# A state-space scan on pairs of channel halves, rows of C read from device memory, and two softplus steps on GpSimd

## The chip, the cores and the metric

The kernel runs on one core of a Trainium2 chip. The metric is the device time of one execution, in microseconds.

## The reference

The input x is four sequences of 512 tokens with 128 channels (2048 columns of 128). Six blocks follow one another, each x + f(LayerNorm(x)): a gated feed-forward net, a state-space mixer, the feed-forward net again, a mixture of experts (64 experts, 8 per token), attention with 8 heads, and the experts again. The change is in the mixer:

```python
xz = x @ in_proj_w.T                       # 2 x 256 channels
x_ssm, z = split(xz)
xc = silu(causal_depthwise_conv4(x_ssm) + conv_b)
xp = xc @ x_proj_w.T                       # 1 + 16 + 16 values per token: dt_r, B, C
dt = softplus(dt_r @ dt_proj_w.T + dt_proj_b)
dA = exp(dt[..., None] * -exp(A_log))      # 256 channels x 16 states
dBx = dt[..., None] * B[:, :, None, :] * xc[..., None]
h_t = dA_t * h_(t-1) + dBx_t               # 512 steps, from 0 in each sequence
y_t = sum over the 16 states of h_t * C_t
y = y + xc * D
out = y * silu(z) @ out_proj_w.T
```

## The kernel before, in words

The kernel is written out by hand for each engine: five instruction streams with semaphores between them. Channels lie on the 128 partitions, tokens along the free dimension. The mixer works on one sequence ("block" i, 0 to 3) of 512 tokens at a time, and its 256 channels are two halves m of 128 partitions.

For a block the work is 16 states n times two halves m, 32 items q = 2n + m. An item takes these steps, all 128 x 512:

- TensorE spreads row n of B over the partitions by a selection matrix (L831), into one of four PSUM banks, three items ahead; for m = 1 it spreads a row of C into bank 2 (L838).
- ScalarE makes exp(dt * A) in `m_da` (L1018, records show `ln_t`), and for m = 1 copies the row of C to `m_c` (L1023).
- VectorE multiplies `du` = dt * xc by the row of B in place in PSUM (L1119), one item ahead, and runs the recurrence over the tokens by one scan instruction into `m_h` (L1126).
- GpSimd multiplies `m_h` by the row of C into `m_hc` (L1181, records show `ln_c`).
- TensorE adds that up over n with an identity matrix, in fp32 (L906).

`m_h`, `m_da` and `m_hc` have four slots of one item (`DEEP`). `scan_items` (L717) interleaves with the items of a block: `ahead`, the work for the next blocks (projections, odd taps of the convolution, silus, low halves, softplus), and `finish`, the end of the block before (y with D, gate, output projection, addition to x). Each stands at a fixed q in the order of every engine. In softplus, ScalarE makes |v|, exp(-|v|) and ln(1 + e) (L983, L987, L991), and VectorE adds max(v, 0) (`softplus_end`, L1090) and multiplies by xc (`dt_times_xc`, L1095), both 128 x 1024. In the last block the LayerNorm of the phase behind is begun as well (`early_centre`, `early_inverse`, `early_normalise` on VectorE). After the last item come the y step (L1152), the gate product (L1158), high and low halves (L234, L237), the output projection and the addition to x (L1165). ScalarE changes its function table between silu, exp, ln and square root (`ACT_TABLE_LOAD`).

An f32r product needs a high and a low half of each operand and three matmuls (`mm3`); a low half is a subtraction (L237). The SP queue issues all DMAs; before the change it has nothing to do during the mixer and waits for the phase's end. `sel_bc` holds the 32 selection matrices. The loops of the scan on VectorE:

```python
def input_term(i, q):
    ...
        bank = ps[:, B_BANKS[q % DEEP], :]
        dve.wait_ge(*M("b_spread", 32 * i + q + 1))
        dve.tensor_tensor(bank, du[:, i % 2, q % MC, :], bank, ALU.mult).then_inc(M["db"], 1)
```

Of the kernel before, what the change touches and what calls it, by code (L numbers as in the profile page):

```python
# [7 lines left out]
P = 128  # L8
T = 512
# [5 lines left out]
MC = 2  # L15
HEADS = 8
# [34 lines left out]
def program(nc, d):  # L51
    ctx = ExitStack()
    with ctx:
# [23 lines left out]
        with ExitStack() as layer:  # L77
# [9 lines left out]
            with ExitStack() as s:  # L87
# [6 lines left out]
                sel_bc = fb("sel_bc", [P, 2 * DS, P], F32R)  # L94
# [10 lines left out]
                m_c = fb("m_c", [P, 2, T])  # L105
# [78 lines left out]
        def group(tag, counts, runs):  # L184
# [24 lines left out]
            "gated g_hi g_lo out x_new aexp bc_zero").split(), 0), 1)  # L209
# [498 lines left out]
        ITEMS = DS * MC  # L708
        DEEP = 4
        B_BANKS, C_BANK, FREE_BANK, SPREAD_AHEAD = (0, 1, 3, 7), 2, 6, 3  # L710
# [6 lines left out]
        def scan_items(item, beside, finish):  # L717

            for i in range(NB):
                for q in range(ITEMS):  # L720
                    item(i, q)
                    if i:
                        finish(i - 1, q)
                    beside(i, q)
            for q in range(13):
                finish(NB - 1, q)
# [48 lines left out]
        def mix_pe(pe, L, N):  # L775
# [48 lines left out]
            def spread_b(i, q):  # L824
                if q >= ITEMS:
                    i, q = i + 1, q - ITEMS
                if i < NB:
                    after(pe, "h", 32 * i + q + 1 - DEEP)
                    if q < SPREAD_AHEAD:
                        pe.wait_ge(*M("bc_lo", i + 1))  # L830
                    pe.matmul(ps[:, B_BANKS[q % DEEP], :], sel_bc[:, q // MC, :], bc[:, cut(i)], start=True, stop=True).then_inc(M["b_spread"], 1)  # L831

            def spread_c(i, n):
                if n >= DS:
                    i, n = i + 1, n - DS
                if i < NB:
                    after(pe, "c_copy", 16 * i + n)
                    pe.matmul(ps[:, C_BANK, :], sel_bc[:, DS + n, :], bc[:, cut(i)], start=True, stop=True).then_inc(M["c_spread"], 1)  # L838

            def ahead(i, q):  # L840

                if i == NB - 1:
                    if q == 0:
                        pe.wait_ge(*M("v", 2 * NB))
                        early_mean(pe, N, 0)
                    if q == 4:
                        pe.wait_ge(*N("centred", 1))
                        early_mean(pe, N, 1)
                    if q == 13:
                        pe.wait_ge(*M("x_new", NB - 1))  # L850
                        early_mean(pe, N, 2)
                    if q == 17:
                        early_vars(pe, N)
                    if q in (22, 25, 28):
                        b = (q - 22) // 3
# [3 lines left out]
                if i + 1 < NB:  # L859
                    if q in (0, 2):  # L860
                        if q == 0:
                            pe.wait_ge(*M("conv", 2 * i + 4))
                        else:
                            pe.wait_ge(*M("sz_raw", 2 * i + 1))
                        z_proj(i + 1, q // 2, FREE_BANK)
                    if q == 14:
                        pe.wait_ge(*M("sz_raw", 2 * i + 2))
                        after(pe, "x_new", i)
                        bc_proj(i + 1, FREE_BANK)
                    if q == 18:  # L870
                        pe.wait_ge(*M("bc_lo", i + 2))
                        dt_proj(i + 1, FREE_BANK)
                if i + 2 < NB:
                    if q == 21:
                        pe.wait_ge(*M("v", 2 * i + 4))
                        pe.wait_ge(*L("xn_lo", i + 3))
                        taps(i + 2, 0, FREE_BANK, False)
                    if q == 23:
# [1461 lines left out]
```

## Time and profile before

| what | us |
|---|---|
| median of three runs | 1674.49 |
| lowest and highest run | 1674.21, 1676.87 |
| the profiled execution | 1673.99 |
| its span, first to last instruction | 1672.1 |
| mean granted TensorE clock in it | 0.986 of full speed |

The profile shows one execution. In its rows PE is TensorE (PEld its weight loads), DVE VectorE, ACT ScalarE, POOL GpSimd and SP the queue that issues DMAs. Idle time before a group of instructions is put down to whatever ended it. A line can be that of a helper, as L234 and L237 (high and low halves) or L229 to L231 (`mm3`). The page cuts the span in 40 slices of 41.8 us; the mixer lies in slices 4 to 11.

### The profile page before, as it was taken

The numbers are of one execution on the slowest core, as the hardware profiler recorded it, in microseconds if no ns is written. First come the engines' busy times: TensorE is split into PE (matmuls) and PEld (weight loads), VectorE is DVE, ScalarE is ACT, GpSimd is POOL, SyncE is SP. The second block draws the span as 40 slices with busy tenths as digits, with TensorE's granted clock in tenths as the row PEclk, the third lists the DMA queues.
The fourth block names the chain that finished last, engine by engine and source line by source line (L and its number), as shares of the span: only waits on it lengthen the run. The fifth ranks groups of instructions, "written<-read, shape, count | busy, mean of one in ns | idle before, by whom it ended". The sixth has DMA issues, their size and how long they took to land.

```text
span 1672.1 us, 23756 instructions
## 1 busy us (share of the span) xinstructions
PE 1575.7 (94%) x7008; PEld 1204.1 (72%) x7008; DVE 1211.4 (72%) x2083; ACT 1061.7 (63%) x2103; POOL 1010.7 (60%) x974
## 2 busy tenths in 40 slices
PE   8999788788899989999999899999998999999998
PEld 6777444344587767877888677878886788778886
DVE  5465798999657646897778568876785688756665
ACT  4344867666334466676778666667786666666665
POOL 1110677867310068987344579884445888878887
PEclk9999899999999999999999999999999999999999
DMA  2000000000000067664200356651003566566763
GB/s 109 24 0 0 1 1 1 1 0 1 26 1 1 1 162 180 174 167 123 51 1 6 87 148 166 173 141 51 1 6 86 140 167 171 151 161 172 172 173 89
DMA packets 58837, 137.36 MB, mean 82 GB/s; under 512 B 10379, under 2 KB 34403, under 8 KB 58467
## 3 DMA queue, kind: packets, MB, share of 16 engines
q1 hardware_dynamic: 58723, 135.99, 31.4%
q8 instruction: 53, 0.87, 0.2%
q14 instruction: 61, 0.50, 0.1%
HBM read 133.86 MB, written 2.10 MB: 81 GB/s over the span
## 4 chain that ended last, share of the span: by engine, by line
PE 65%; POOL 5%; ACT 5%; issue 4%; DVE 2%; DMA 1%; PEldq 0%; SPq 0%; POOLq 0%; PEld 0%; ACTq 0%; DVEq 0%
PE ps L229 19%; PE ps L230 18%; PE ps L231 18%; POOL ln_c L1181 4%; PE ps L1789 2%; PE ps L1774 1%; PE ps L1776 1%; PE ps L1775 1%; DMA e_raw<-in_experts 1%; PE ps L906 1%; ACT e_s L1390 1%; ACT e_hi L234 1%; PE ps L1777 1%; PE ps L372 0%; ACT L248 0%
## 5 line engine op out<-in xcount | busy, mean ns | idle before, releaser
L237 POOL TENSOR_TENSOR e_lo<-e_h,e_hi 128x512 fp32r<-128x512 f32 (+1 forms) x368 | 475.9, 1294 | 151.4 <-ACT e_hi L234 140.9
L1569 DVE TENSOR_TENSOR ps<-e_s,ps 128x512 f32<-128x512 f32 x352 | 244.8, 695 | 188.0 <-PE ps L231 139.9
L1390 ACT ACTIVATE e_s<-ps 128x512 f32<-128x512 f32 (+1 forms) x368 | 219.9, 598 | 238.2 <-PE ps L231 233.6
L229 PE MATMUL ps<-xn_hi,eh 128*128 128x512 f32 x704 | 285.0, 405 | 19.9 <-ACT e_s L1390 17.6
L230 PE MATMUL ps<-xn_lo,eh 128*128 128x512 f32 x704 | 281.2, 399 | 0.0
L231 PE MATMUL ps<-xn_hi,el 128*128 128x512 f32 x704 | 280.1, 398 | 0.0
L1574 DVE TENSOR_TENSOR e_h<-ps,rwb 128x512 f32<-128x512 f32 x352 | 243.3, 691 | 16.7 <-DVE ps L1569 2.2
L234 ACT ACTIVATE e_hi<-e_h 128x512 fp32r<-128x512 f32 (+1 forms) x368 | 229.3, 623 | 5.5 <-DVE e_h L1574 3.2
L237 POOL TENSOR_TENSOR el<-e_raw,eh 128x128 fp32r<-128x128 f32 (+1 forms) x352 | 219.9, 626 | 17.6 <-ACT eh L1375 17.6
L1181 POOL TENSOR_TENSOR ln_c<-m_h,m_c 128x512 f32<-128x512 f32 x128 | 168.5, 1320 | 66.4 <-DVE m_h L1126 63.4
L229 PEld LDWEIGHTS ps<-xn_hi,eh 128*128 128x128 f32 x704 | 133.2, 189 | 64.2 <-issue 13.3
L906 PE MATMUL ps<-ln_c,const 128*128 128x512 f32 x256 | 143.4, 643 | 25.3 <-POOL ln_c L1181 19.9
L1126 DVE TENSOR_TENSOR_SCAN m_h<-ln_t,ps 128x512 f32<-128x512 f32 x128 | 154.9, 1210 | 2.4 <-ACT ln_t L1018 2.3
L231 PEld LDWEIGHTS ps<-xn_hi,el 128*128 128x128 f32 x704 | 133.4, 189 | 31.4
L230 PEld LDWEIGHTS ps<-xn_lo,eh 128*128 128x128 f32 x704 | 133.3, 189 | 29.1 <-issue 1.0
L229 PE MATMUL ps<-e_hi,eh 128*128 128x512 f32 x352 | 139.9, 397 | 0.0
L230 PE MATMUL ps<-e_lo,eh 128*128 128x512 f32 x352 | 139.6, 397 | 0.0
L237 POOL TENSOR_TENSOR xn_lo<-ln_c,xn_hi 128x512 fp32r<-128x512 f32 x21 | 30.9, 1472 | 179.2 <-ACT xn_hi L234 179.2
L231 PE MATMUL ps<-e_hi,el 128*128 128x512 f32 x352 | 138.8, 394 | 0.0
L229 PE MATMUL ps<-hid_hi,wh 128*128 128x512 f32 x288 | 120.6, 419 | 3.5 <-DVE hid_lo L237 2.7
L231 PE MATMUL ps<-hid_hi,wl 128*128 128x512 f32 x288 | 113.3, 394 | 0.0
L230 PE MATMUL ps<-hid_lo,wh 128*128 128x512 f32 x288 | 113.3, 393 | 0.0
(276 smaller groups left out, 3228.0 us busy)
## 6 DMA issues: line engine op xcount, KB each, us to landing
e_raw<-in_experts SPq DMA_DIRECT2D x176, 192.0 KB, 3.9
rwb<-rw_rows SPq DMA_DIRECT2D x64, 352.0 KB
rwb<-rw_rows SPq DMA_DIRECT2D x80, 256.0 KB
rwb<-rw_rows SPq DMA_DIRECT2D x32, 320.0 KB
rwb<-rw_rows SPq DMA_DIRECT2D x48, 192.0 KB
rwb<-rw_rows SPq DMA_DIRECT2D x32, 224.0 KB
rwb<-rw_rows SPq DMA_DIRECT2D x32, 160.0 KB
rwb<-rw_rows SPq DMA_DIRECT2D x80, 64.0 KB
```

The lines of the kernel that those rows point to most:

```text
L229: pe.matmul(out, w_hi, x_hi, start=start, stop=False, skip_group_check=True)
L230: pe.matmul(out, w_hi, x_lo, start=False, stop=False, skip_group_check=True)
L231: return pe.matmul(out, w_lo, x_hi, start=False, stop=stop, skip_group_check=True)
L234: return act.activation(hi, full, ACT.Identity)
L237: return eng.tensor_tensor(lo, full, hi.bitcast(F32), ALU.subtract)
L906: pe.matmul(ps[:, 4 + m, :], ident, m_hc[:, q % DEEP, :], start=(n == 0), stop=(n == DS - 1), skip_group_check=True).then_inc(M["y_sum"], 1)
L1126: dve.tensor_tensor_scan(m_h[:, q % DEEP, :], m_da[:, q % DEEP, :], ps[:, B_BANKS[q % DEEP], :], 0.0, ALU.mult, ALU.add).then_inc(M["h"], 1)
L1181: pool.tensor_tensor(m_hc[:, q % DEEP, :], m_h[:, q % DEEP, :], m_c[:, n % 2, :], ALU.mult).then_inc(M["hc"], 1)
L1390: act.activation(e_s[0:rows_, buf, :], ps[0:rows_, bank, :], ACT.Silu).then_inc(S["silu"], 1)
L1569: dve.tensor_tensor(ps[:, bank, :], e_s[:, buf, :], ps[:, 5, :], ALU.mult).then_inc(S["gated"], 1)
L1574: dve.tensor_tensor(e_h[:, buf, :], ps[:, bank, :], rwb[:, c, cut(b)], ALU.mult).then_inc(S["weighted"], 1)
L1789: last = pe.transpose(pt_at(kb)[:, (r - kb) * P:(r - kb + 1) * P], p32[:, r, kb * P:(kb + 1) * P], ident)
```

## The change

The loop now runs over the 16 states with both halves in one instruction of 1024 elements. `m_h`, `m_da`, `m_hc` are used as two slots of a pair. The scan runs through both halves as one line of 1024; exp(dt * A) of the first token of half 1 is set to 0 once (`da_zero`), which starts that half afresh. The row of B is spread once for both halves, into the single bank 7, and the product goes to banks 0, 1 or 2, 3. C isn't spread by TensorE any more: the 32 projected rows are also kept as plain fp32 (`bc_full`), the 16 rows of C are stored to device memory, and SP loads each row back to all 128 partitions into a ring of four (`m_c`). For blocks 1 to 3, ScalarE makes max(v, 0) (`positive`) and GpSimd adds the logarithm and multiplies by xc, one half at a time. The steps beside the loop get new places n, and z of block 0 goes through the common path. The core of the diff:

```diff
+C_RING = 4
-                sel_bc = fb("sel_bc", [P, 2 * DS, P], F32R)
+                sel_bc = fb("sel_bc", [P, DS, P], F32R)
-                m_c = fb("m_c", [P, 2, T])
+                m_c = fb("m_c", [P, C_RING, T])
+                bc_f = fb("bc_f", [2 * DS, T])
...
+        B_BANK, FREE_BANK = 7, 6
+        def two(k):
+            return slice(MC * (k % 2), MC * (k % 2) + MC)
...
@@ TensorE @@
+            def spread_b(i, n):
...
+                    after(pe, "db", DS * i + n)
+                    if n == 0:
+                        pe.wait_ge(*M("bc_lo", i + 1))
+                    pe.matmul(ps[:, B_BANK, :], sel_bc[:, n, :], bc[:, cut(i)], start=True, stop=True).then_inc(M["b_spread"], 1)
-            def spread_c(i, n):
...
+            def side(i, n):
+                if i + 1 < NB:
+                    if n == 4:
...
+                        bc_proj(i + 1, FREE_BANK)
+                    if n == 5:
...
+                        dt_proj(i + 1, FREE_BANK)
+                    if n == 6:
...
+                        z_proj(i + 1, 0, FREE_BANK)
+                    if n == 7:
...
+                        z_proj(i + 1, 1, FREE_BANK)
+                    if n == 9 and i:
...
+                        out_proj(i - 1)
+                if i + 2 < NB:
+                    if n == 10:
...
+                        taps(i + 2, 0, FREE_BANK, False)
...
+            def item(i, n):
+                spread_b(i, n + 2)
+                if n:
+                    side(i, n)
+                    total(i, n - 1)
...
@@ ScalarE @@
+            def item(i, n):
...
+                after(act, "h", DS * i + n - 1)
+                for m in range(MC):
+                    act.activation(m_da[:, MC * (n % 2) + m, m:T], dt[:, i % 2, m, m:T], ACT.Exp,
+                                   scale=neg_a[:, m * DS + n:m * DS + n + 1]).then_inc(M["da"], 1)
+            def side(i, n):
...
+                if n == 1:
+                    if i + 1 < NB:
+                        x_silu(i + 1)
+                    z_silu(i)
...
+                    if n == 5:
+                        bc_high(i + 1, FREE_BANK)
+                        bc_full(i + 1, FREE_BANK)
...
+                    if n == 9:
+                        softplus_abs(i + 1)
+                        softplus_exp(i + 1)
+                    if n == 10:
+                        softplus_ln(i + 1)
+                        positive(i + 1)
...
+                if i == NB - 1:
...
+                    if n == 13:
+                        for b in range(NB - 1):
+                            early_deviation(act, N, b)
...
@@ VectorE @@
+            def input_term(i, n):
...
+                    dve.wait_ge(*M("b_spread", DS * i + n + 1))
+                    after(dve, "h", DS * i + n - 1)
+                    dve.tensor_tensor(ps[:, two(n), :], du[:, i % 2, :, :], of_both(ps[:, B_BANK, :]), ALU.mult).then_inc(M["db"], 1)
...
+            def item(i, n):
+                input_term(i, n + 1)
+                if n == 1 and i:
+                    y_linear(i - 1)
+                if n == 5 and i + 1 < NB:
+                    bc_low(i + 1, FREE_BANK)
+                dve.wait_ge(*M("da", 32 * i + 2 * n + 2))
+                dve.wait_ge(*M("db", DS * i + n + 1))
+                after(dve, "hc", DS * i + n - 1)
+                dve.tensor_tensor_scan(in_line(m_h[:, two(n), :]), in_line(m_da[:, two(n), :]), in_line(ps[:, two(n), :]), 0.0,
                                        ALU.mult, ALU.add).then_inc(M["h"], 1)
+            def side(i, n):
+                if i and n == 9:
+                    x_add(i - 1)
+                if i + 2 < NB and n in (11, 14):
+                    odd_taps(i + 2, (n - 11) // 3, FREE_BANK)
                 if i == NB - 1:
...
+                    if n == 12:
+                        for b in range(NB - 1):
+                            early_inverse(dve, N, b)
+                    if n >= 13:
+                        early_normalise(dve, N, n - 13)
...
@@ GpSimd @@
+            def item(i, n):
+                pool.wait_ge(*M("h", DS * i + n + 1))
+                pool.wait_ge(*M(f"c_in{n % C_RING}", 16 * (DS // C_RING * i + n // C_RING + 1)))
+                after(pool, "y_sum", 32 * i + 2 * n - 2)
+                pool.tensor_tensor(m_hc[:, two(n), :], m_h[:, two(n), :], of_both(m_c[:, n % C_RING, :]), ALU.mult).then_inc(M["hc"], 1)
...
+            def step_sum(i, m):
...
+                pool.tensor_tensor(dt[:, i % 2, m, :], dt[:, i % 2, m, :], du[:, i % 2, m, :], ALU.add).then_inc(M["dt"], 1)
+            def step_times_xc(i, m):
...
+                pool.tensor_tensor(du[:, i % 2, m, :], dt[:, i % 2, m, :], xc[:, i % 3, m, :], ALU.mult).then_inc(M["du"], 1)
+            def side(i, n):
+                if i + 1 < NB:
+                    if n in (10, 11):
+                        step_sum(i + 1, n - 10)
+                    if n == 12:
+                        step_times_xc(i + 1, 0)
+                        step_times_xc(i + 1, 1)
+                if i + 1 < NB and n in (1, 2):
+                    x_low(i + 1, n - 1)
+                if i and n in (3, 4):
...
+            scan_pairs(item, side)
+            for b in range(NB - 1):
+                early_low(pool, N, b)
+        def mix_load_c(sp):
+            def store(i):
+                sp.wait_ge(*M("bc_full", i + 1))
+                sp.dma_start(d["c_rows"][:, cut(i)], bc_f[DS:2 * DS, :]).then_inc(M["c_out"], 16)
+            store(0)
+            for i in range(NB):
+                sp.wait_ge(*M("c_out", 16 * (i + 1)))
+                for n in range(DS):
+                    after(sp, "hc", DS * i + n + 1 - C_RING)
+                    sp.dma_start(m_c[:, n % C_RING, :], d["c_rows"][n:n + 1, cut(i)].broadcast_to([P, T])).then_inc(M[f"c_in{n % C_RING}"], 16)
+                    if n == 11 and i + 1 < NB:
+                        store(i + 1)
```

## Rows read from the trace of the kernel before

**Rows 1.** window view, state-space stage (us, busy us per engine, TensorE clock)

```profile
180.00:432.00 252.00, 212.84 (x604) 108.68 (x603) 240.94 (x288) 173.79 (x264) 191.62 (x148) 0.96 0.00 1
```

**Rows 2.** groups by line, 120-450 us (busy us, mean ns; idle before)

```profile
L1181 POOL TENSOR_TENSOR ln_c<-m_h,m_c 128x512 f32<-128x512 f32 x128 | 168.5, 1320 | 66.4 <-DVE m_h L1126 63.4 <-issue 2.0 <-PE ps L906 0.9
L1126 DVE TENSOR_TENSOR_SCAN m_h<-ln_t,ps 128x512 f32<-128x512 f32 x128 | 154.9, 1210 | 2.4 <-ACT ln_t L1018 2.3
...
L1119 DVE TENSOR_TENSOR ps<-du,ps 128x512 f32<-128x512 f32 x128 | 86.5, 677 | 6.0 <-PE ps L831 5.9
...
L1018 ACT ACT_TABLE_LOAD x8 | 10.3, 1283 | 0.9 <-DVE dt L1090 0.8
...
L1095 DVE TENSOR_TENSOR du<-dt,xc 128x1024 f32<-128x1024 f32 x4 | 4.8, 1204 | 0.0
...
L983 ACT ACTIVATE du<-dt 128x1024 f32<-128x1024 f32 x4 | 4.2, 1054 | 0.0
```

**Rows 3.** timeline, VectorE: start us, us, engine line operation

```profile
282.90 1.21 DVE L1126 TENSOR_TENSOR_SCAN m_h<-ln_t,ps 128x512 f32<-128x512 f32 x1
...
284.61 1.21 DVE L1126 TENSOR_TENSOR_SCAN m_h<-ln_t,ps 128x512 f32<-128x512 f32 x1
```

**Rows 4.** waits of VectorE, 179 to 440 us (total us, times, longest)

```profile
DVE ps L1119 <- PE ps L831: 5.9, 4, 2.2
DVE x L1165 <- PE ps L231: 3.0, 3, 1.2
...
DVE m_h L1126 <- ACT ln_t L1018: 2.3, 2, 1.2
```

**Rows 5.** timeline, GpSimd, beside the softplus sum on VectorE

```profile
295.03 2.19 POOL L1181 TENSOR_TENSOR ln_c<-m_h,m_c 128x512 f32<-128x512 f32 x1 [1.03 <-DVE m_h L1126]
297.88 1.28 POOL L1181 TENSOR_TENSOR ln_c<-m_h,m_c 128x512 f32<-128x512 f32 x1 [0.65 <-DVE m_h L1126]
```

**Rows 6.** timeline, VectorE, instructions that wait for their predecessor

```profile
444.83 0.43 DVE L658 CAST hid_hi<-f_h 128x512 fp32r<-128x512 f32 x1
445.29 0.69 DVE L237 TENSOR_TENSOR hid_lo<-f_h,hid_hi 128x512 fp32r<-128x512 f32 x1
```

**Rows 7.** groups by line and form, GpSimd, whole span

```profile
L2242 POOL TENSOR_TENSOR m_h<-m_h,m_raw 128x1024 f32<-128x1024 f32 x1 | 2.4, 2402 | 4.9 <-DVE hid_lo L237 4.9
```

**Rows 8.** timeline, TensorE (x2: two records of one fp32 product)

```profile
268.45 0.39 PE L231 MATMUL ps<-g_hi,ml 128*128 128x512 f32 x1
268.68 0.40 PE L831 MATMUL ps<-bc,sel_bc 128*128 128x512 f32 x1
...
270.24 1.02 PE L906 MATMUL ps<-ln_c,const 128*128 128x512 f32 x2
...
271.56 1.02 PE L906 MATMUL ps<-ln_c,const 128*128 128x512 f32 x2
```

**Rows 9.** timeline, VectorE, first products and last scan of the stage

```profile
179.71 1.29 DVE L1119 TENSOR_TENSOR ps<-du,ps 128x512 f32<-128x512 f32 x2
...
429.53 1.21 DVE L1126 TENSOR_TENSOR_SCAN m_h<-ln_t,ps 128x512 f32<-128x512 f32 x1
```

**Rows 10.** timeline, GpSimd and VectorE, after the last scan

```profile
431.56 1.26 POOL L1181 TENSOR_TENSOR ln_c<-m_h,m_c 128x512 f32<-128x512 f32 x1
...
434.71 1.29 DVE L1158 TENSOR_TENSOR m_y<-m_y,sz 128x512 f32<-128x512 f32 x2
```

**Rows 11.** timeline, VectorE, a cast beside a GpSimd step (feed-forward phase)

```profile
141.53 1.51 DVE L658 CAST hid_hi<-f_h 128x512 fp32r<-128x512 f32 x1
```

**Rows 12.** DMA issues of the page: x times, KB each, median us to landing

```profile
e_raw<-in_experts SPq DMA_DIRECT2D x176, 192.0 KB, 3.9
...
const<-in_const SPq DMA_DIRECT2D x1, 400.0 KB, 10.3
```

**Rows 13.** window view, 424 to 430 and 196 to 202 us

```profile
424.00:430.00 6.00, 4.10 (x12) 1.37 (x10) 6.00 (x8) 1.54 (x4) 5.28 (x5) 1.00 0.00 0
196.00:202.00 6.00, 3.46 (x7) 1.67 (x6) 4.92 (x6) 5.97 (x10) 4.95 (x5) 0.74 0.01 1
```

More of the change, by code:

```diff
@@ L715, in after, with scan_pairs @@
                 eng.wait_ge(*M(name, n))
-        def scan_items(item, beside, finish):
+        def scan_pairs(item, side):
             for i in range(NB):
[L720 to L726, printed above, removed]
+                for n in range(DS):
+                    item(i, n)
+                    side(i, n)
         def normed_early(b):
@@ L909, in finish, with total @@
[L909 to L925 removed]
+            def total(i, n):
+                for m in range(MC):
+                    if n == 0:
+                        after(pe, "ylin", 2 * i + m - 1)
+                        if i == 0:
+                            pe.wait_ge(*M("sz_raw", MC - m))
+                    if m == 0:
+                        pe.wait_ge(*M("hc", DS * i + n + 1))
+                    pe.matmul(ps[:, 4 + m, :], ident, m_hc[:, MC * (n % 2) + m, :], start=(n == 0), stop=(n == DS - 1),
+                              skip_group_check=True).then_inc(M["y_sum"], 1)
@@ L1025, in ahead @@
-            def ahead(i, q):
+            def item(i, n):
+                if n == 0:
+                    act.wait_ge(*M("dt", 2 * i + 2))
+                    if i == 0:
+                        act.wait_ge(*M("da_zero", 1))
+                after(act, "h", DS * i + n - 1)
+                for m in range(MC):
+                    act.activation(m_da[:, MC * (n % 2) + m, m:T], dt[:, i % 2, m, m:T], ACT.Exp,
+                                   scale=neg_a[:, m * DS + n:m * DS + n + 1]).then_inc(M["da"], 1)
@@ L1053, in ahead @@
-                if i + 2 < NB:
-                    if q == 24:
-                        x_raw(i + 2, 0, FREE_BANK)
-                    if q == 30:
-                        x_raw(i + 2, 1, FREE_BANK)
-            def finish(i, q):
-                if q == 0 and i == NB - 1:
-                    early_high(act, N, NB - 2)
-                if q == 9:
-                    after(act, "out", i)
-                    for m in range(MC):
-                        act.wait_ge(*M("gated", 2 * i + m + 1))
-                        split_hi(act, g_hi[:, m, :], m_y[:, m, :]).then_inc(M["g_hi"], 1)
@@ L1068, in mix_act, with gate_high @@
-            scan_items(item, ahead, finish)
+                    if n == 15:
+                        early_high(act, N, 0)
+            def gate_high(i):
+                after(act, "out", i)
+                for m in range(MC):
+                    act.wait_ge(*M("gated", 2 * i + m + 1))
+                    split_hi(act, g_hi[:, m, :], m_y[:, m, :]).then_inc(M["g_hi"], 1)
+            scan_pairs(item, side)
+            early_high(act, N, 1)
+            early_high(act, N, 2)
+            gate_high(NB - 1)
@@ new lines, in mix_dve @@
+            input_term(0, 0)
+            scan_pairs(item, side)
+            i = NB - 1
+            y_linear(i)
+            dve.wait_ge(*M("sz", 2 * i + 2))
+            for m in range(MC):
+                dve.wait_ge(*M("ylin", 2 * i + m + 1))
+                dve.tensor_tensor(m_y[:, m, :], m_y[:, m, :], sz[:, i % 3, m, :], ALU.mult).then_inc(M["gated"], 1)
+            for m in range(MC):
+                dve.wait_ge(*M("g_hi", 2 * i + m + 1))
+                split_lo(dve, g_lo[:, m, :], m_y[:, m, :], g_hi[:, m, :]).then_inc(M["g_lo"], 1)
```

329 lines of the change are left out of this document (114 added, 215 removed).

## The prediction

> **What bounds the kernel now.** I read the page's 40 slices first: the state-space stage fills the fifth to the eleventh, and the change touches nothing else. The window view of that stage comes next [rows 1]: of 252.0 us VectorE is busy 240.9, TensorE 212.8, GpSimd 191.6, ScalarE 173.8, and DMA idles. So VectorE sets the pace. The groups by line [rows 2] say what it does: 128 scans of 1210 ns and 128 products of 677 ns. Their sum, 1.89 us, overstates the cost, since neighbours overlap: the timeline has scans starting 1.71 us apart (282.90, 284.61) with a product between [rows 3]. The stage runs from the first product at 179.71 to the last scan's end at 429.53 + 1.21 = 430.74 [rows 9], 251.0 us. VectorE's own accounting of it: 128 x 1.71 = 218.9; its small steps, in the stage, at duration less the 0.085 overlap (677 + 1210 less 1710 is 177 ns in two joints): six y steps of 0.65 = 3.9, three x additions, three low halves of B, four odd-tap additions, and six LayerNorm steps, 16 of about 0.6 = 9.6, three reciprocals 0.3, together 13.8; softplus sum and product by the input for three blocks, each 1024 wide like L1095, 6 x 1.12 = 6.7 [rows 2]. That is 239.4, and 11.6 are left for waits. The waits view gives 5.9 for the B spreads, 2.3 for ScalarE's exponentials, 3.0 for x (one of its three waits lies in the tail) [rows 4]. Last, the chain of waits follows GpSimd's product with C through most of the stage; it is on the chain only because each waits for the scan before it, with 63 us idle before it [rows 2], so it isn't the bound.
>
> **The change, part by part.**
>
> 1. **Pairs.** 64 scans and 64 products of 1024 elements replace 128 and 128 of 512. The 1024-wide product: 1204 ns, the row of the same operation and width (L1095) [rows 2]. The wide scan isn't in the trace. Its per-element part is (1210 - 144)/512 = 2.08 ns, with 144 ns fixed from the product's two widths (677 and 1204), so 1210 + 1066 = 2276 ns; bounds: 2 x 1210 = 2420 if nothing is saved, 2276 - 144 = 2132 if part of the fixed time is also spared. I take 2276, which both widths of its neighbour support. But a wait is added: product n+1 writes the banks that scan n-1 reads, so it waits for the scan just ahead of it on its own engine. Instructions that wait for their predecessor start 0.03 us after its end (444.83 + 0.43, then 445.29) [rows 6] and no longer 0.085 before it. A pair thus costs 1.204 - 0.085 + 2.276 + 0.03 = 3.43 us, against 2 x 1.71 = 3.42. Joining the halves gives VectorE nothing: 64 x 3.43 = 219.5, that is +0.6. If that wait were free it would be 3.31, -7.4 in all; with a 2420 scan +9.2.
>
> 2. **Softplus sum and product to GpSimd.** VectorE loses 6.7. GpSimd gets 12 products of 1.28 and ScalarE three 1024-wide rectifications of 1.05, the row of its absolute value (L983) [rows 2]. GpSimd had a second cost before: a product beside the VectorE softplus step took 2.19 us (295.03) instead of 1.28 (297.88) [rows 5]. The Trainium skill (SBUF — State Buffer, Who interferes with whom) says that a VectorE instruction with two SBUF inputs shuts out a GpSimd instruction that reads SBUF for its whole length; the trace agrees, and by that rule nothing in the new loop collides, for its scans and products have one operand in PSUM.
>
> 3. **GpSimd.** The wide product with C: 2.40 us, the 1024-wide product [rows 7], 2.35 issued back to back. Per block 16 x 2.35 plus at most 10 steps of 1.24 is 50 us, under VectorE's 57. In pairs with a step it needs 3.6 against 3.43, so it lags by 0.2, and by 1.4 at n = 12, where two steps stand. The products by the input are then ready about 1 us before the next block's first product wants them. Cost nothing; without that cover, 1 to 2 us in each of three blocks.
>
> 4. **TensorE.** 64 B spreads and all 64 C spreads go. Back to back an f32r product takes 0.23 (268.45, 268.68); a y sum is 1.32 - 2 x 0.23 = 0.86 (270.24 to 271.56 with two spreads between) [rows 8]. A pair costs 0.23 + 1.72 = 1.95, with six side products 3.33: under 3.43, barely. The single B bank makes spread n+1 wait for product n, and it stands behind y sum n-3. It is ready some 2.1 us after product n starts, and VectorE wants it after 3.4. Slack 1.3: nothing. At the very first pair there is no scan to hide it: the second product waits 0.9 (a spread's 0.40, twice that at the low clock after an idle stretch, and 0.1 for the two signals).
>
> 5. **ScalarE.** 64 copies of C go, and with them its coupling to GpSimd, which kept it from running ahead. Its worst stretches are table load, four silus, table load, or load, logarithm, rectification, load (loads of 1283 ns) [rows 2]; I place their ends 1.1 to 1.3 us before the scan that needs them. The 2.3 of waits go, and the spread and x waits right behind them, caused by the same delay. New: in the last block the square root stands at n = 13 on ScalarE while VectorE takes its reciprocals at n = 12: load 1.28, three small steps, about 2.0 of wait. I allow 2.4 more for the bc, odd-tap and x hand-overs, eight of about 0.3. Waits: 4.4 instead of 11.6, -7.2.
>
> 6. **C by DMA.** 64 issues on SP of one row to 128 partitions, 256 KB each, and four stores. A 192 KB load lands in 3.9 us [rows 12]; 256 KB in proportion 5.2; bounds 3.9 and 10.3, the 400 KB load in a crowd [rows 12]. A slot of the ring of four is free 11 us before its product (4 x 3.43 less 2.40). Cost nothing. Behind these issues on SP stand only loads that wait for the stage's end anyhow. The first row can start some 8 us ahead of its use.
>
> 7. **Start.** The odd-tap addition no longer stands between softplus sum and product: -0.5. With the 0.9 of part 4: +0.4.
>
> 8. **Tail.** After the last scan now: product with C 2.40 and two y sums, where it was 1.26, begun at 431.56, with one sum [rows 10]. Before, the gate product began 434.71 - 430.74 = 3.97 after the scan's end. Now 0.1 + 2.40 + 1.2 + 0.86 to the second sum, + 0.7 for its y step = 5.3: +1.35. And three low halves now follow on GpSimd, busy to 6.2, when the gate product (two SBUF inputs) wants to start. A VectorE cast beside such a GpSimd step took 1.51 [rows 11] for 0.43 [rows 6]; I take 0.9. Bounds 0 and 1.1. Tail +2.25.
>
> **Sum:** work +0.6 - 6.7 = -6.1; start +0.4; waits -7.2; tail +2.25: -10.65. The profiled execution took 1673.99 (span 1672.1), which is 0.5 under the median 1674.49. 1673.99 - 10.65 = 1663.3; against the median 1663.8. I say 1664.
>
> **Rivals.**
>
> **The waits stay.** The hand-overs through one B bank and rings of two cost as much as the old ones: then only work, start and tail count, -3.45, 1671. For it: VectorE has no reserve left in the loop. Against: the slacks above. 0.17.
>
> **The wait is free or the wide scan cheaper.** The joint costs what it did: -7.4 more, 1656. Against: the two rows of joints. 0.08.
>
> **Slower: GpSimd becomes the bound.** Place: the wide product with C. If the broadcast operand or the row landing in SBUF spares it nothing and costs what a collision costs [rows 5], it takes 2 x 1.28 + 0.91 = 3.47, and with 30 steps of 1.24 GpSimd needs 64 x 3.47 + 37 = 259 for the stage, against 238 forecast for VectorE with its waits: +21, and 1.1 in the tail, 1686. It decides from (238 - 37)/64 = 3.1 us, and makes the kernel slower than before from 3.3. For it: GpSimd's rows do stretch, and rings of two can't carry a lag. Against: nothing with two SBUF inputs is left beside it, and the 1024-wide row is 2.40. 0.10.
>
> **TensorE's clock.** TensorE idles about 1.5 us in every quiet pair. At 1.2 GHz a pair costs 3.44 + 0.46 = 3.9, 0.47 over VectorE, 64 times +30: 1694. Against: in 424 to 430, sums 1.71 apart and 4.10 of 6 us busy, the granted clock was 1.00; it fell to 0.74 where busy time was 3.46 [rows 13]. The Trainium skill (TensorE: Matmul & The Clock Gate, A second HAM failure mode: psum-queue depth-cycling) tells of a kernel whose frequent short idles made the clock swing between its levels; by it TensorE would be at the low level about half the time, some +15, 1679. 0.04.
>
> **How the numbers follow.** Forecast 0.61, own range 1659 to 1669 (waits 0 to 9). Slower than before: the last two, 0.14, of which 0.01 comes out near no change. A measurement of this kernel can tell 0.2%, 3.3 us, from no change. The 1671 case straddles that: half same, and 0.07 of the forecast's upper edge. So faster 0.71, same 0.16, slower 0.13. The range 1657 to 1674 leaves out the last two rivals and the edge of the second.
>
> **What would show it.** Right: scans of about 2.28 us starting 3.43 apart, product directly after scan with no overlap; GpSimd's product 2.4; almost no VectorE wait for B spreads or exponentials; about 2 us before the reciprocals; the gate product 6 us after the last scan. Wrong: VectorE waits for spreads in most pairs (first rival), a joint under 0 (second), GpSimd at 3.1 or more, or a granted clock under 0.9 over the stage.

## The result and the profile after

| | before | after |
|---|---|---|
| median, us (five runs each) | 1675.80 | 1664.32 |
| lowest and highest | 1674.21, 1678.73 | 1662.22, 1667.44 |
| profiled execution, span | 1673.99, 1672.1 | 1664.32, 1662.5 |
| after / before | | 0.9949, interval 0.9930 to 0.9968 |

The changed kernel is 0.5% faster: 1664.3 against 1664.0 forecast. The sum behind the forecast is tested on the mixer alone, cut at four marks that every trace has: its first matmul, VectorE's first product, the end of the last scan and the end of the last addition to x. "Waits" are the idle times that the timeline shows ahead of VectorE's instructions between the second and the third mark, the stage.

| us | to first product | stage | waits in it | tail | mixer |
|---|---|---|---|---|---|
| before | 23.97 | 251.03 | 10.0 | 8.62 | 283.62 |
| after | 23.61 | 239.98 | 3.55 | 10.54 | 274.13 |
| difference | -0.36 | -11.05 | -6.5 | +1.92 | -9.49 |
| forecast | -0.5 | -12.4 | -6.3 | +2.25 | -10.65 |

The stage's -12.4 is work -6.1, waits -7.2 and the 0.9 of the very first pair. The forecast counted the waits of before as what its accounting left, 11.6, so its waits after are 4.4 + 0.9 = 5.3; its column shows 5.3 - 11.6. What lies outside the mixer differs from one profiled execution to the next (1386.7 to 1390.6 us in those shown here, 1393.4 in that of the last run), so small effects are read from the mixer's marks and the medians only confirm them.

The window view of the stage, columns as in [rows 1]; the second line is its first 12 us:

```profile
180.00:421.00 241.00, 190.18 (x475) 83.40 (x476) 232.29 (x154) 148.62 (x212) 185.47 (x94) 0.94 0.23 68
180.00:192.00 12.00, 5.49 (x8) 2.37 (x8) 10.87 (x8) 11.93 (x18) 4.46 (x2) 0.50 0.36 60
```

VectorE is busy 232.3 of 241.0 us and still sets the pace; TensorE has lost 23 us, ScalarE 25, GpSimd 6. DMA, at 0.00 before, is at 0.23. The groups by line and form, 120 to 445 us [rows 2]:

```profile
L1181 POOL TENSOR_TENSOR ln_c<-m_h,m_c 128x1024 f32<-128x1024 f32 x64 | 151.7, 2371 | 62.9 <-DVE m_h L1142 60.0 <-PE ps L909 2.9
L1142 DVE TENSOR_TENSOR_SCAN m_h<-ln_t,ps 128x1024 f32<-128x1024 f32 x64 | 145.9, 2279 | 0.1
...
L1121 DVE TENSOR_TENSOR ps<-du,ps 128x1024 f32<-128x1024 f32 x64 | 78.6, 1227 | 7.2 <-PE ps L837 1.8 <-DVE m_h L1142 0.5
```

The scan of both halves takes 2.279 us (2.276 forecast), the product 1.227 (1.204), GpSimd's product 2.371 (2.40). A joint is here the passage from one instruction to the next on the same engine: below 0 when the two overlap, above 0 when there is a gap. The idle time before L1121 shows how a joint hides: 7.2 us in all, of which 1.8 and 0.5 are put down to somebody. The rest is in slivers of 0.1, and the timeline of VectorE shows them (columns as in [rows 3]):

```profile
187.54 2.28 DVE L1142 TENSOR_TENSOR_SCAN m_h<-ln_t,ps 128x1024 f32<-128x1024 f32 x1
189.93 1.23 DVE L1121 TENSOR_TENSOR ps<-du,ps 128x1024 f32<-128x1024 f32 x1
191.06 2.28 DVE L1142 TENSOR_TENSOR_SCAN m_h<-ln_t,ps 128x1024 f32<-128x1024 f32 x1
193.45 1.23 DVE L1121 TENSOR_TENSOR ps<-du,ps 128x1024 f32<-128x1024 f32 x1
...
223.59 2.28 DVE L1142 TENSOR_TENSOR_SCAN m_h<-ln_t,ps 128x1024 f32<-128x1024 f32 x1
225.79 0.66 DVE L1080 TENSOR_TENSOR xc<-ps,xc 128x511 f32<-128x511 f32 x1
226.37 1.22 DVE L1121 TENSOR_TENSOR ps<-du,ps 128x1024 f32<-128x1024 f32 x1
```

A scan ends at 189.82, and the product that waits for it begins at 189.93: +0.11. Scans start 3.52 apart, where 3.43 was forecast and two items of before took 3.42. Where a small step lies between scan and product, it begins 0.08 before the scan's end (223.59 + 2.28 = 225.87, then 225.79), and so does the product behind it. Fifty joints of the stage are of the first kind, 12 of the second.

VectorE's waits from 181 to 421 us are these [rows 4]:

```profile
DVE ps L1121 <- PE ps L837: 1.8, 3, 0.9
DVE rstd L759 <- ACT rstd L771: 1.3, 1, 1.3
DVE ps L1121 <- DVE m_h L1142: 0.5, 1, 0.5
```

One spread wait of 0.9 is the very first pair's. The waits for ScalarE's exponentials and for the x addition are gone. The end of the stage, answering [rows 9, 10]:

```profile
418.47 2.28 DVE L1142 TENSOR_TENSOR_SCAN m_h<-ln_t,ps 128x1024 f32<-128x1024 f32 x1
...
420.82 2.35 POOL L1181 TENSOR_TENSOR ln_c<-m_h,m_c 128x1024 f32<-128x1024 f32 x1 [0.42 <-DVE m_h L1142]
...
425.57 1.28 POOL L239 TENSOR_TENSOR xn_lo<-dt,xn_hi 128x512 fp32r<-128x512 f32 x1
425.91 2.09 DVE L1166 TENSOR_TENSOR m_y<-m_y,sz 128x512 f32<-128x512 f32 x2
```

The two gate products start 5.16 us after the last scan's end (420.75; before 3.97) and take 2.09 together instead of 1.29, beside a low half on GpSimd. The DMA issues [rows 12]:

```profile
m_c<-c_rows SPq DMA_DIRECT2D x64, 256.0 KB, 3.1
```

In the chain that ended last, GpSimd's product had 4% of the span before; now VectorE's scan has 7% and that product 1%.

### The profile page after: what moved, and what is told of

Same layout as the page of the kernel before. It is cut to its first block, busy times and chain, and to the rows that moved or that the text cites. A ratio compares the mean times of both kernels' runs of the same rounds, so it can differ in the third digit from the quotient of the medians.

```text
span 1662.5 us, 23216 instructions
## 1 busy us (share of the span) xinstructions
PE 1557.2 (94%) x6880; PEld 1182.2 (71%) x6880; DVE 1203.8 (72%) x1952; ACT 1035.0 (62%) x2048; POOL 1007.1 (61%) x922
## 4 chain that ended last, share of the span: by engine, by line
PE 66%; DVE 11%; issue 5%; ACT 4%; POOL 2%; DMA 1%; PEldq 0%; SPq 0%; POOLq 0%; DVEq 0%; PEld 0%; ACTq 0%
PE ps L231 19%; PE ps L232 19%; PE ps L233 19%; DVE m_h L1142 7%; PE ps L1816 2%; DVE ps L1121 1%; PE ps L1801 1%; PE ps L1802 1%; PE ps L1803 1%; POOL ln_c L1181 1%; PE ps L909 1%; ACT e_hi L236 1%; PE ps L1804 1%; ACT e_s L1417 1%; DMA e_raw<-in_experts 0%
## 5 line engine op out<-in xcount | busy, mean ns | idle before, releaser
L231 PE MATMUL ps<-xn_hi,eh 128*128 128x512 f32 x704 | 284.5, 404 | 18.1 <-ACT e_s L1417 14.7
L1181 POOL TENSOR_TENSOR ln_c<-m_h,m_c 128x1024 f32<-128x1024 f32 x64 | 151.7, 2371 | 62.9 <-DVE m_h L1142 60.0
L231 PEld LDWEIGHTS ps<-xn_hi,eh 128*128 128x128 f32 x704 | 132.9, 189 | 61.9 <-ACT e_s L1417 11.5
L909 PE MATMUL ps<-ln_c,const 128*128 128x512 f32 x256 | 132.1, 640 | 21.8 <-POOL ln_c L1181 21.8
L1142 DVE TENSOR_TENSOR_SCAN m_h<-ln_t,ps 128x1024 f32<-128x1024 f32 x64 | 145.9, 2279 | 0.1
L1015 ACT ACTIVATE ln_t<-dt,neg_a 128x512 f32<-128x512 f32 (+1 forms) x128 | 85.2, 713 | 62.9 <-DVE m_h L1142 62.2
```

The costliest lines, as they stand in the source:

```text
L231: pe.matmul(out, w_hi, x_hi, start=start, stop=False, skip_group_check=True)
L909: pe.matmul(ps[:, 4 + m, :], ident, m_hc[:, MC * (n % 2) + m, :], start=(n == 0), stop=(n == DS - 1), skip_group_check=True).then_inc(M["y ...
L1015: act.activation(m_da[:, MC * (n % 2) + m, m:T], dt[:, i % 2, m, m:T], ACT.Exp, scale=neg_a[:, m * DS + n:m * DS + n + 1]).then_inc(M["da" ...
L1142: dve.tensor_tensor_scan(in_line(m_h[:, two(n), :]), in_line(m_da[:, two(n), :]), in_line(ps[:, two(n), :]), 0.0, ALU.mult, ALU.add).then_ ...
L1181: pool.tensor_tensor(m_hc[:, two(n), :], m_h[:, two(n), :], of_both(m_c[:, n % C_RING, :]), ALU.mult).then_inc(M["hc"], 1)
```

## The experiments

My theory was that VectorE gained by losing the softplus steps and its waits, and nothing by the pairs. A near hit does not show that, since several terms could be off against each other. The first four runs add parts of the change to the kernel before, three more change one thing in the kernel after, and the last four go after what the pairs cost. Each ratio is to the runs of before taken with it. It need not equal the quotient of the medians: for the first run that is 1691.19/1673.61 = 1.0105.

**A wait on the predecessor, alone.** Edit on the kernel before: every product also waits for the scan just ahead of it on VectorE, which the data doesn't need.

```diff
                     dve.wait_ge(*M("b_spread", 32 * i + q + 1))
+                    after(dve, "h", 32 * i + q - 1)
```

> The kernel before, with one more wait: each product (L1119) waits for the scan just ahead of it on VectorE, as in the change. Theory (the joint between an instruction and a successor that waits for it is dear): the joint scan to product goes from -0.09 us to +0.11 us, as in the changed kernel's trace (191.06 + 2.28, then 193.45), in about 108 of 128 places where no small step lies between: +18 to +22 us, 1692 to 1697. Rival (the 0.11 belongs to the wide instructions or their broadcast operand, and a wait alone costs 0.03 as between 444.83 and 445.29): 108 x 0.12 = +13 at most, 1687; or nothing, if the gap is a matter of the wide form alone: 1675.

Median 1691.19, ratio 1.0086 (1.0062 to 1.0111); the stage takes 268.50, +17.5. The timeline of VectorE:

```profile
205.12 1.21 DVE L1127 TENSOR_TENSOR_SCAN m_h<-ln_t,ps 128x512 f32<-128x512 f32 x1
206.44 0.70 DVE L1120 TENSOR_TENSOR ps<-du,ps 128x512 f32<-128x512 f32 x1
207.04 1.21 DVE L1127 TENSOR_TENSOR_SCAN m_h<-ln_t,ps 128x512 f32<-128x512 f32 x1
```

Scans start 1.92 apart where it was 1.71 [rows 3]: the joint goes from -0.085 to +0.11, and the product from 0.68 to 0.70. So the price belongs to the wait, not to the width. In 97 places a product stands straight behind a scan: there the joint goes from -0.082 to +0.105, 97 x 0.187 = 18.1 us, and 128 products 0.017 longer are 2.2. The slower items also ran into fewer waits (6.9 for 10.0), which gives 3.1 back: 17.2 of the 17.5.

**Rows of C by DMA, alone.** Items stay as they were; TensorE's spreads and ScalarE's copies of C go, with store, loads and ring of four as in the change.

```diff
-                    act.activation(m_c[:, n % 2, :], ps[:, C_BANK, :], ACT.Identity).then_inc(M["c_copy"], 1)
...
+                    sp.dma_start(m_c[:, n % C_RING, :], d["c_rows"][n:n + 1, cut(i)].broadcast_to([P, T])).then_inc(M[f"c_in{n % C_RING}"], 16)
```

> The kernel before, items of one half, with the rows of C from device memory in a ring of four rows (no C spread on TensorE, no copy on ScalarE). Theory (ScalarE's coupling to GpSimd through that copy caused its lateness, and that caused VectorE's waits for exponentials, B spreads and x, 9.7 us of them in the stage): 6 to 9 us less, 1666 to 1669. Rival (those waits come from the order of the small steps and stay): within 2 us of before, 1673 to 1676. A third, that the DMA is late or disturbs something: GpSimd or VectorE wait for it, slower than before.

Median 1669.05, ratio 0.9969 (0.9957 to 0.9981); stage 244.62, -6.4, waits 3.7 instead of 10.0. ScalarE's waits, first of before, 180 to 432 us:

```profile
ACT ln_t L1018 <- DVE m_h L1126: 32.0, 37, 1.9
ACT m_c L1023 <- POOL ln_c L1181: 31.0, 41, 1.4
```

and in this run, 180 to 426 us:

```profile
ACT ln_t L1015 <- DVE m_h L1121: 86.1, 76, 2.5
```

Before, ScalarE stood 41 times for GpSimd to free a slot of C. Now, ahead of its exponentials, it waits for VectorE alone (76 times), so it is ahead by all that its slots allow, and VectorE has no wait for exponentials left. How one late copy of C reached VectorE, the trace of before shows (TensorE, then VectorE; below that the window view, columns as in [rows 1]):

```profile
263.33 0.50 PE L838 MATMUL ps<-bc,sel_bc 128*128 128x512 f32 x1 [3.22 <-ACT m_c L1023]
265.98 0.70 DVE L1119 TENSOR_TENSOR ps<-du,ps 128x512 f32<-128x512 f32 x1 [1.94 <-PE ps L831]
```

```profile
264.00:267.00 3.00, 3.00 (x6) 1.35 (x4) 1.06 (x3) 3.00 (x6) 3.00 (x3) 0.50 0.00 0
```

Behind two table loads and four silus on ScalarE, TensorE idled 3.22 us for the copy, came back at a granted clock of 0.50 (1.2 GHz), and the next spread of B kept VectorE waiting 1.94. The edit takes away three things at once: the wait for GpSimd, 64 copies on ScalarE (0.58 us each) and 64 spreads on TensorE. The runs do not separate them.

**Softplus steps on GpSimd, alone.** The sum stands at q = 24 and 25, the product by the input at q = 26 and 27, on the kernel before.

```diff
+                if i + 1 < NB and q in (24, 25):
+                    step_sum(i + 1, q - 24)
+                if i + 1 < NB and q in (26, 27):
+                    step_times_xc(i + 1, q - 26)
```

> The kernel before, with softplus sum and its product with xc for blocks 1 to 3 on GpSimd (24 to 27 of 32 items) and max(v, 0) on ScalarE. Theory (VectorE sets the pace and loses 6 x 1.12 us): 5 to 7 us less, 1668 to 1670. Rival (GpSimd's steps in a row hold up the y sums, and ScalarE's extra step its exponentials, so that VectorE waits instead): 0 to 3 us less.

Median 1673.88, ratio 1.0000 (0.9988 to 1.0012). VectorE lost 6.7 us of work, but the stage only 1.75 (249.28): the shown waits rose from 10.0 to 14.2. VectorE's waits, 180 to 430 us, then the same run's first of ScalarE, then rows of the timeline:

```profile
DVE ps L1123 <- PE ps L831: 8.7, 9, 2.0
DVE m_h L1130 <- ACT ln_t L1021: 3.3, 5, 1.2
```

```profile
ACT m_c L1026 <- POOL ln_c L1181: 32.5, 38, 2.2
```

```profile
290.99 1.04 ACT L990 ACTIVATE dt<-dt 128x1024 f32<-128x1024 f32 x1
294.09 1.22 DVE L1130 TENSOR_TENSOR_SCAN m_h<-ln_t,ps 128x512 f32<-128x512 f32 x1 [0.33 <-ACT ln_t L1021]
295.21 0.50 PE L838 MATMUL ps<-bc,sel_bc 128*128 128x512 f32 x1 [2.38 <-ACT m_c L1026]
299.32 0.70 DVE L1123 TENSOR_TENSOR ps<-du,ps 128x512 f32<-128x512 f32 x1 [0.59 <-PE ps L831]
```

The new waits stand in every block behind the third part of this edit, the max(v, 0) on ScalarE. It takes 1.04 us between the logarithm and the table load; the exponentials and the copy of C behind the load come 0.9 later than before, VectorE waits 0.33 for the first of them, and TensorE 2.38 for the copy; it has no gap from there on, with six side products among its work, and two of its spreads come 0.59 and 0.34 late. In the third block the same chain ends in a wait of 1.15, at a granted clock of 0.50. GpSimd has no gap from 292 to 303 us either and is late (ScalarE's copy of C waits up to 2.2 for it, before 1.4), but the first such wait of this block, 0.22 at 299.74, comes after the waits of 0.33 and 0.59. The edit cost VectorE as waits most of what it saved it as work. No run has the steps on GpSimd without the step on ScalarE.

**Both, on items of one half.** The two edits together: the whole change except the pairs and what came with them (the single bank of B, the new places of the steps beside the loop, z of block 0 on the common path).

> The two edits together (C by DMA, softplus steps on GpSimd), still on items of one half: the change without its pairs. Theory (pairs gain nothing on VectorE, since a pair costs 3.53 us against 3.42, and cost 1.9 us in the tail): 12 to 16 us less than before, 1659 to 1663, 2 to 6 us faster than the changed kernel. Rival (the pairs are what makes it fast, by fewer waits): 1665 or more.

Median 1662.67, ratio 0.9931 (0.9910 to 0.9951); stage 235.90, -15.1. Alone the parts gave 6.4 and 1.75: together they give 7 more than their sum. With the copies of C gone, ScalarE has a lead again and its extra step makes nobody wait: behind that edit the softplus move is worth 8.7, of which 6.7 is the work and 1.7 fewer waits (3.7 to 2.0). VectorE's waits left from 180 to 417 us:

```profile
DVE ps L1118 <- PE ps L833: 1.1, 1, 1.1
DVE m_y L1147 <- PE ps L900: 0.9, 1, 0.9
DVE x L1160 <- PE ps L233: 0.8, 2, 0.4
```

This kernel's stage is 4.1 us shorter than the changed kernel's, and its tail 1.9 (8.60). A later run shows that 0.8 of those 1.9 belong to the order of GpSimd's low halves and not to the pairs.

**Softplus back on VectorE, in the kernel after.** The six steps of GpSimd go; VectorE has its two again, at n = 12 and 13.

```diff
+                if i + 1 < NB and n == 12:
+                    softplus_end(i + 1)
+                if i + 1 < NB and n == 13:
+                    dt_times_xc(i + 1)
```

> The changed kernel with softplus sum (n = 12) and product with xc (n = 13) back on VectorE, and no rectification on ScalarE. Theory (VectorE sets the pace in the changed kernel too): three blocks of 2 x 1.12 = +6.7, less 0.2 to 0.3 for each joint that a step now covers, +5.5: 1669 to 1671; GpSimd's product with C takes 3.3 beside them instead of 2.37. Rival (GpSimd's row of four steps is what holds VectorE up at a block's end): +2 at most, 1666.

Median 1670.17, ratio 0.9978 (0.9965 to 0.9992); stage 246.34, +6.4, its waits 3.9, hardly more than the 3.55. So VectorE's work does set the pace of the changed kernel, at 6.4 for 6.7. GpSimd, beside the two steps (which run from 289.29 and from 293.73):

```profile
285.55 2.38 POOL L1184 TENSOR_TENSOR ln_c<-m_h,m_c 128x1024 f32<-128x1024 f32 x1 [1.14 <-DVE m_h L1141]
289.45 3.27 POOL L1184 TENSOR_TENSOR ln_c<-m_h,m_c 128x1024 f32<-128x1024 f32 x1 [1.53 <-DVE m_h L1141]
293.90 3.25 POOL L1184 TENSOR_TENSOR ln_c<-m_h,m_c 128x1024 f32<-128x1024 f32 x1 [1.18 <-DVE m_h L1141]
```

**Roots one state earlier, last low half behind the gate.**

```diff
-                    if n == 13:
+                    if n == 12:
                         for b in range(NB - 1):
                             early_deviation(act, N, b)
...
             for b in range(NB - 1):
+                if b == NB - 2:
+                    pool.wait_ge(*M("g_lo", 2 * NB))
                 early_low(pool, N, b)
```

> The changed kernel with two small edits: the square roots at n = 12 on ScalarE instead of 13, and GpSimd's last low half only after VectorE's last low half. Theory: the wait of 1.27 us before the reciprocals goes down by at most 0.4, since ScalarE waits for the sums of squares in either case; the gate products go from 2.09 back to 1.29 us. Together 0.8 to 2 us, 1662 to 1664. Rival (the 2.09 is not a collision with GpSimd's low half but the operation's own time there): gate products stay at 2.09.

Median 1664.96, ratio 0.9944 (0.9922 to 0.9965). The tail half came as expected, the gate products from 2.09 to 1.29 and the tail from 10.54 to 9.76:

```profile
425.55 1.29 DVE L1166 TENSOR_TENSOR m_y<-m_y,sz 128x512 f32<-128x512 f32 x2
```

The other half won nothing. Two of VectorE's waits, 181 to 422 us:

```profile
DVE m_h L1142 <- ACT ln_t L1015: 1.3, 1, 1.3
...
DVE rstd L759 <- ACT rstd L771: 1.3, 1, 1.3
```

The reciprocals still wait 1.3, and now the scan behind them waits 1.3 for the exponentials, which stand on ScalarE behind the roots and the load of their own table. Stage +1.1, nothing won in all.

**A ring of two for C.** `C_RING = 2` instead of 4.

> The changed kernel with a ring of two rows of C instead of four. Theory (a row lands in 3.1 us, and a slot is then free 2 x 3.52 - 2.37 = 4.7 us before its product): no change within 1 us, GpSimd never waits for a DMA, 1664. Rival (the shown 3.1 us hides issue and queueing): GpSimd waits by up to 1 us a pair, 64 times, up to 1720.

Median 1664.17, ratio 0.9942 (0.9925 to 0.9959); stage 240.08, waits 3.55: no change. GpSimd's waits:

```profile
POOL ln_c L1181 <- DMA m_c<-c_rows: 7.1, 3, 2.5
```

Against my expectation GpSimd did wait for rows, 7.1 us in three places (with four slots it never did), and none of it reached VectorE. The loads are covered with half the slots.

**Two scans of one half, with the next product between them.** The scan of half 0, then the wide product, then the scan of half 1, so that no product waits for its direct predecessor. The low half stays behind the gate, as above.

```diff
+                for m in range(MC):
+                    k = MC * (n % 2) + m
+                    dve.wait_ge(*M("da", 32 * i + 2 * n + m + 1))
+                    dve.tensor_tensor_scan(m_h[:, k, :], m_da[:, k, :], ps[:, k, :], 0.0, ALU.mult, ALU.add).then_inc(M["h"], 1)
+                    if m == 0:
+                        input_term(i, n + 1)
```

> The changed kernel with each wide scan cut in two of 512 and the wide product of the next pair between them, so that no instruction of the loop waits for the one just ahead of it; GpSimd's last low half also waits for VectorE's. Theory (the joint costs 0.11 us where the predecessor is waited for and -0.09 where it isn't): a pair costs 1.14 + 2 x 1.12 = 3.39 us instead of 3.53, the stage 239.98 - 7.3 = 232.7 us, the tail 9.8; some 8 us under the changed kernel, 1655 to 1658, in spite of 64 more scans. Rival (one more instruction per pair costs its fixed 0.14 us, or the later product makes TensorE's B spread late): no faster than the changed kernel, 1664 or more.

Median 1664.70, ratio 0.9940 (0.9916 to 0.9964), where 1655 to 1658 was expected: the rival came true. The joint is gone:

```profile
190.59 2.32 DVE L1139 TENSOR_TENSOR_SCAN m_h<-ln_t,ps 128x512 f32<-128x512 f32 x2
192.83 1.21 DVE L1121 TENSOR_TENSOR ps<-du,ps 128x1024 f32<-128x1024 f32 x1
193.95 2.32 DVE L1139 TENSOR_TENSOR_SCAN m_h<-ln_t,ps 128x512 f32<-128x512 f32 x2
```

A pair takes 3.36 us instead of 3.52, yet the stage takes 240.89: the waits went from 3.55 to 10.2. The two largest, 181 to 422 us, and the place of one on TensorE and VectorE:

```profile
DVE x L1131 <- PE ps L233: 2.6, 3, 0.9
DVE rstd L759 <- ACT rstd L771: 2.3, 1, 2.3
```

```profile
272.78 1.21 DVE L1121 TENSOR_TENSOR ps<-du,ps 128x1024 f32<-128x1024 f32 x1
...
274.05 0.50 PE L837 MATMUL ps<-bc,sel_bc 128*128 128x512 f32 x1 [0.95 <-DVE ps L1121]
...
275.54 0.40 PE L233 MATMUL ps<-g_hi,ml 128*128 128x512 f32 x1
...
275.97 0.69 DVE L1131 TENSOR_TENSOR x<-x,ps 128x512 f32<-128x512 f32 x1 [0.86 <-PE ps L233]
```

The spread can't start before the product ends at 273.99, and six side products stand behind the spread; the x addition comes one scan later and finds them unfinished. The scans between product and side step were the cover, and half of it was moved away.

**The two contenders again, on one chip.** The kernel after and the one with items of one half, unchanged.

> The changed kernel as it is, on the same chip as the two others of this call, for a direct comparison: 1662 to 1665, stage 240.0, tail 10.5.

> The kernel without pairs (C by DMA, softplus steps on GpSimd) again, on the same chip: theory (pairs cost more than they gain) stage 235.9, tail 8.6, 3 to 6 us under the changed kernel; rival (the earlier difference of the two medians, 1.6 us with overlapping intervals, was chance): within 1 us of it.

Medians 1664.86 (12 runs) and 1661.64 (6 runs), ratios to the same runs of before 0.9954 (0.9938 to 0.9971) and 0.9929 (0.9905 to 0.9953). Those intervals overlap, but the marks repeat to 0.4 us: mixer 273.85 and 268.51 (stages 239.66 and 235.85), in the first traces 274.13 and 268.52. The mixer is 5.3 us shorter without the pairs; 3.2 of it shows in the medians.

**Side products ahead of the spread.** On the kernel with two half scans, TensorE makes a pair's side products first and then the spread. The first product for the next phase's LayerNorm gets a wait for its input of its own, since the old order no longer gives it.

```diff
-                spread_b(i, n + 2)
                 if n:
                     side(i, n)
+                spread_b(i, n + 2)
+                if n:
                     total(i, n - 1)
```

> The kernel of e8, with TensorE's order in an item turned round: the small step's products first, then the B spread two pairs on, then the y sums. In e8 the spread waits for a product that VectorE now makes 1.1 us later, and the small step's products stand behind it, while VectorE reaches its own part of the hand-over earlier. Theory (those hand-overs are where the shorter loop's 7 us went): VectorE's waits in the stage fall from 10.2 to 3 to 5 us, the stage from 240.9 to 234 to 236, the whole to 1657 to 1660. Rival (the waits have other causes, ScalarE's lateness or the y sums): stage within 2 us of 240.9, 1663 or more.

Median 1660.95, ratio 0.9920 (0.9903 to 0.9938). Stage 233.12, tail 9.75, mixer 266.51: 7.6 shorter than the changed kernel's and the shortest of all. Its three largest waits, 181 to 414 us:

```profile
DVE m_h L1142 <- ACT ln_t L1018: 1.1, 1, 1.1
DVE m_h L1142 <- issue: 1.0, 1, 1.0
DVE rstd L759 <- ACT rstd L771: 0.7, 1, 0.7
```

The x and odd-tap waits are gone, and the shorter pair counts at last. Against items of one half the mixer is 2.0 us shorter (the stage by 2.8, the tail is 1.2 longer); whole times (0.9920 and 0.9929) can't tell those two apart. Of the 7.6 us in the mixer only 3.4 shows in the medians. In this run's profile the rest of the kernel took 1393.4 us where the changed kernel's took 1388.4, and the granted clock of its six executions was 0.980 to 0.985, where those of items of one half had 0.984 to 0.991. Whether the new order causes that is open.

## Why the prediction was right

The range held, the likeliest case came true, and the number is 0.3 us off. That it is so near is luck: the median of before alone lay between 1672.7 and 1675.8 in the five groups of runs, and two errors in the sum cancel in part. The gain itself is 8.5 us by the ratio, 11.5 by the medians and 9.5 by the mixer's marks, where 10.65 was forecast. Step by step:

1. **Pairs: mechanism right, price too low.** That pairs give VectorE nothing came out, for the reason given: the wait on the predecessor takes what the halved count saves. The term that was mis-sized is the joint: taken as +0.03 from a cast and its low half [rows 6], it measured +0.11. With the product 0.02 longer a pair took 3.52 for 3.43, on 50 pairs +4.5; where a small step lies between, the joint overlaps and the pair takes 3.33, on 12 pairs -1.2. With the ends (two products up to the first scan, 2 x 1.14, and the last two scans, 2.20 + 2.28) that is 176.0 + 40.0 + 6.8 = 222.8 in place of 64 x 3.43 = 219.5: +3.3. Adding the small steps, 13.8, and the waits, 3.55, gives 240.1, and the stage took 239.98. The row I took the joint from is of two other operations; the run with the added wait shows the price where it counts, behind a scan. Two slips are small: the fixed part of the product, 2 x 677 - 1204, is 150 ns and not 144 (0.4 us over all scans), and the 11.6 us called waits of before hold 1.6 us of work that 1.71 an item misses, since the timeline shows 10.0.
2. **Softplus to GpSimd:** 6.7 forecast, 6.4 when put back. But on the kernel before, this step alone gave 1.75; by the rows of that run, ScalarE had no lead for the max(v, 0) that comes with it. The prediction listed it as a saving of its own; it is one only behind the change to C.
3. **GpSimd** had reserve: 2.37 a product and no wait of VectorE for it. The rival with GpSimd as the bound at 3.1 or more is refuted; a product took more than that (3.27) only in the run where VectorE's two-input step stood beside it.
4. **TensorE:** the 0.9 of the very first pair came out at 0.89. The slack of 1.3 for the other spreads held at the full clock only: two of them made VectorE wait 0.29 and 0.64, each beginning in a stretch with a granted clock of 0.50. The prediction had put them at nothing.
5. **Waits:** 5.3 forecast, 3.55 measured. The roots cost 1.3, not 2.0. The hand-overs of bc, odd taps and x, allowed 2.4, cost nothing: no such wait is in the view. What stands in their place is the 0.93 of the two spreads and 0.46 before one product, which the view puts down to the scan ahead of it. That the change to C removes the waits is shown by C by DMA alone: that part gives 6.4 by itself. That it does so by setting ScalarE free of GpSimd is read from the waits and not tested apart from the copies and spreads that go with it. The first rival (waits stay) is refuted.
6. **C by DMA** costs nothing, not even with two slots, and a row lands in 3.1 us, not 5.2.
7. **Start and tail:** -0.36 for -0.5. Tail +1.92 for +2.25: the gate starts 1.2 later (1.35 forecast) and takes 0.8 more (0.9). Moving the low half gives that 0.8 back, so the collision is shown. The Trainium skill (SBUF — State Buffer, Who interferes with whom) has the rule that was used here, that a VectorE instruction with two SBUF inputs and a GpSimd one that reads SBUF contend; both traces agree (2.09 for 1.29, 3.27 for 2.38).

So two terms erred against each other, work +3.3 and waits -1.8, and the sum of the mixer was off by 1.2 of 10.65. What the prediction did not ask is whether all parts belong in the sum. They don't: without the pairs, and the single bank and new places that came with them, the other parts give 15.1 in the stage; with them 4.1 is lost again there and 1.9 in the tail.

The rival of TensorE's clock was priced for a whole stage at 1.2 GHz, +30, or for half of it, +15; the half was an assumption, and no row gave it. The clock did fall, to 0.50 in five stretches that make 26 of the stage's 240 us (0.94 over the stage; before, 23 of 251 us), and besides the 0.89 of the very first pair the waits that begin in them add up to 0.93.

## What to carry to other kernels

When instructions are merged to save their fixed cost, look at which one then has to wait for its direct predecessor on its own engine: the joint lost (0.2 us here) can be as large as the cost saved, and putting an independent step between gets both. A part that moves work off the bounding engine pays only if every engine that gets something for it (here ScalarE too) can be late without anybody's operands being late; test parts alone and together, since here they gave 6.4 and 1.75 alone and 15.1 together. And a wait shortened in one place shows up behind the next instruction of the late engine, as with the roots, so look at what else stands in that engine's queue before moving it.

## What the runs showed of the hardware that was not expected

- **Waiting for the scan just ahead costs a product on VectorE about 0.2 us.** Independent neighbours overlap by 0.08 to 0.09; a product that waits for the scan just ahead begins 0.11 after it ends, at 512 wide (206.33, then 206.44) as at 1024. The cast and low half of [rows 6], 0.03 apart, were no guide to it.
- **The TensorE clock fell again and again, and cost little.** In the stage's first 12 us TensorE was busy 5.5 and the granted clock 0.50, 1.2 GHz. Four records of y sums took 3.75 us there (188.89) and 1.96 soon after (192.87), yet VectorE's scans started 3.52 apart: the low clock cost nothing after the very first pair. Later in the stage the clock fell to 0.50 again at 237.4, 312.5, 356.9 and 370.5 us, each time for a few us, and each time TensorE had idled 1.7 to 2.1 us shortly before. In the first and the third of these VectorE's waits of 0.29 and 0.64 begin. The third, in the window view and VectorE's timeline:

```profile
357.00:360.00 3.00, 3.00 (x5) 1.19 (x4) 2.82 (x2) 0.84 (x3) 1.79 (x1) 0.50 0.29 92
```

```profile
360.46 1.23 DVE L1121 TENSOR_TENSOR ps<-du,ps 128x1024 f32<-128x1024 f32 x1 [0.64 <-PE ps L837]
```

In the kernel before, all four of VectorE's waits for spreads (5.9 us, at 202.4, 266.0, 331.7 and 410.4) begin inside such a stretch, the largest three after TensorE had stood 2.5 to 3.2 us for ScalarE's copy of C. How much of them is the clock and how much the idle time, no run separates. The Trainium skill (TensorE: Matmul & The Clock Gate, A second HAM failure mode: psum-queue depth-cycling) tells of a clock that swings at frequent short idles; this trace agrees in kind.
- **One row to 128 partitions.** 256 KB landed in 3.1 us, faster than the 192 KB of expert weights in 3.9 [rows 12].
